# Routing rows in a fused attention and mixture-of-experts kernel: scatters queued ahead of gathers, late rows cleared by plain transfers, and a new split of the last sums

## The reference

```python
x = x + xattn(_layernorm(x), ctx_512, W_k, b_k, ln_gamma, ln_beta)   # softmax of a normalised similarity
...
xf = _layernorm(x).reshape(-1, 256)
top_vals, top_idx = jax.lax.top_k(xf @ router_w.T + router_b, 4)
rw = jax.nn.softmax(top_vals, axis=-1) * 1.8
combine = einsum('tke,tk->te', one_hot(top_idx, 32), rw)
g = silu(einsum('th,eih->tei', xf, gate_w));  u = einsum('th,eih->tei', xf, up_w)
routed = einsum('tei,ehi,te->th', g * u, down_w, combine)
shared = (silu(xf @ shared_gate_w.T) * (xf @ shared_up_w.T)) @ shared_down_w.T
x = x + routed + shared
```

## Time and profile before

| what | us |
|---|---|
| median of 3 runs (lowest and highest) | 178.49 (177.79, 180.09) |
| the profiled execution | 178.13 |
| its span in the trace | 176.0 |
| PE busy | 160.0 |
| DVE busy | 103.1 |
| POOL busy | 82.2 |
| ACT busy | 69.2 |

### The profile page before, as it was taken

How to read it: one execution, slowest core, us unless ns; L and a number is a source line. 1 busy time by engine, 2 the same in 40 slices (tenths; PEclk the granted TensorE clock), 3 DMA queues, 4 the chain that set the end, 5 groups by cost and what they waited for, 6 DMA issues and landing times.

```text
span 176.0 us, 3525 instructions
## 1 busy us (share of the span) xinstructions
PE 160.0 (91%) x1113; PEld 122.9 (70%) x1113; DVE 103.1 (59%) x366; ACT 69.2 (39%) x217; POOL 82.2 (47%) x97
## 2 busy tenths in 40 slices
PE   1999999789989889994998998999999969999993
PEld 0355545356868689994897996899999955338881
DVE  3568598879888426861963776642334434326570
ACT  2024587699765442333033221332234542450020
POOL 6031100000005777787777777774777777710000
PEclk9999999999999999999699999999999999999999
DMA  2899999998991489999469799999999843239964
GB/s 73 243 323 384 326 369 304 343 340 282 295 360 50 113 243 324 334 327 311 153 182 301 219 334 337 299 366 360 352 332 364 248 151 113 93 104 404 406 219 134
DMA packets 22346, 47.60 MB, mean 270 GB/s; under 512 B 3764, under 2 KB 12914, under 8 KB 21682
## 3 DMA queue, kind: packets, MB, share of 16 engines
q1 hardware_dynamic: 18194, 37.35, 64.4%
q0 software_dynamic: 3584, 9.44, 15.6%
q10 hardware_dynamic: 544, 0.52, 0.9%
HBM read 40.44 MB, written 6.86 MB: 269 GB/s over the span
## 4 chain that ended last, share of the span: by engine, by line
PE 40%; POOL 26%; DMA 11%; issue 11%; ACT 7%; DVE 4%; DVEq 0%; POOLq 0%
DMA y_d<-y,to 9%; POOL y_d L485 7%; POOL xn L479 7%; POOL xnT L479 7%; PE ps_x L843 3%; PE ps_g L1010 3%; PE ps_g L836 3%; POOL added_weight L494 2%; DMA xn<-rows_d,idx 2%; PE ps_g L1121 2%; PE ps_h L1121 2%; PE ps_g L1128 2%; POOL y_d L490 2%; PE ps_y L1024 1%; PE ps_y L1026 1%
## 5 line engine op out<-in xcount | busy, mean ns | idle before, releaser
L479 POOL DMA_INDIRECT xn<-rows_d,idx x20 | 20.4, 1021 | 39.1 <-DVE idx L1439 33.3
L485 POOL DMA_INDIRECT y_d<-y,to x32 | 32.7, 1022 | 11.2 <-issue 8.5
L993 PEld LDWEIGHTS ps_g<-xgT,wgu 128*128 128x128 f32 x256 | 31.0, 192 | 1.9 <-ACT xgT L703 0.8
L993 PE MATMUL ps_g<-xgT,wgu 128*128 128x128 f32 x256 | 31.4, 276 | 0.6 <-ACT xgT L703 0.6
L1570 DVE COPY y<-ps_y 128x256 f32<-128x256 f32 x36 | 14.8, 423 | 26.3 <-DMA y_d<-y,to 20.3
L709 ACT ACTIVATE gate<-ps_g 128x256 f32<-128x256 f32 x16 | 6.1, 384 | 50.2 <-PE ps_g L993 50.2
L479 POOL DMA_INDIRECT xnT<-rows_d,idx x16 | 15.4, 964 | 4.9 <-issue 4.6
L993 PE MATMUL ps_h<-xgT,wgu 128*128 128x128 f32 x128 | 16.9, 275 | 0.0
L703 ACT ACTIVATE xgT<-ps_x 128x256 f32<-128x256 f32 x36 | 12.3, 382 | 9.7 <-PE ps_x L979 8.9
L993 PEld LDWEIGHTS ps_h<-xgT,wgu 128*128 128x128 f32 x128 | 15.6, 192 | 0.0
L1024 PE MATMUL ps_y<-wda,hT 128*128 128x256 f32 x32 | 10.0, 428 | 3.4 <-DVE y L1570 3.4
(11 more groups left out here) (265 smaller groups left out, 306.6 us busy)
## 6 DMA issues: line engine op xcount, KB each, us to landing
wgu<-in_w_gu SPq DMA_DIRECT2D x28, 384.0 KB, 4.8
wgu<-in_w_gu SPq DMA_DIRECT2D x5, 1536.0 KB, 13.8
wda<-in_w_da SPq DMA_DIRECT2D x29, 128.0 KB, 5.3
wgu<-y_d SPq DMA_DIRECT2D x6, 512.0 KB, 6.8
wda<-in_w_da SPq DMA_DIRECT2D x5, 512.0 KB, 14.3
wdb<-in_w_db SPq DMA_DIRECT2D x29, 64.0 KB, 5.8
wdb<-in_w_db SPq DMA_DIRECT2D x10, 128.0 KB, 15.5
xnT<-in_xT SPq DMA_DIRECT2D x2, 512.0 KB, 6.4
```

The source lines that it names most:

```text
L479: g.indirect_dma_start(xg[j % RING], None, rows_d, bass.IndirectOffsetOnAxis(ap=idx[:, j:j + 1], axis=0)).then_inc(gathered[j % RING], 16)
L485: g.indirect_dma_start(y_d, bass.IndirectOffsetOnAxis(ap=to[:, j:j + 1], axis=0), y[:, j % 4, :], None).then_inc(scattered[j % 4], 16)
L993: last = t.matmul(bank[:, to_col + i * P:to_col + (i + 1) * P], w_up(2 * m + i, c)[:, at:at + P], xgT[:, i, c, :], start=(c == 0), stop=(c ...
```

## The change

On GpSimd: LEAD goes from 8 to 6, so 12 gathers stand ahead of the loop, and inside the loop the two scatters of pair m come before the two gathers of pair m+6. The four indirect scatters of zeros are gone. In their place SP issues three plain transfers that write zeros over all route rows of the token tiles 5, 6 and 7 (512 KB each), after the second gather has landed, and GpSimd waits for them ahead of its first scatter. The four gathers of weights are split in two and two, and so are the one-hot matrices on DVE. At the end DVE sums five token tiles and PE three, ACT makes one set of diagonal matrices less, and all four output transfers come from SP.

```diff
-LEAD = 8
+LEAD = 6
...
-ON_PE = (1, 3, 5, 7)
+ON_PE = (1, 5, 7)
+ON_DVE = (0, 2, 3, 4, 6)
...
+            sp.wait_ge(gathered[1], 16)
+            yv = y_d[0:ROUTES, :].rearrange("(p k c) h -> p k c h", p=P, c=TOPK)
+            for k in range(EARLY, NT):
+                sp.dma_start(yv[:, k, :, :], wide[:, :].bitcast(F32).unsqueeze(1).to_broadcast([P, TOPK, H])).then_inc(zeroed, 16)
             sp.wait_ge(w4_ready, 1)
...
-            sp.wait_ge(zeroed, 16 * ADDED)
...
-            for q in range(2, 4):
-                sp.wait_ge(final, q + 1)
-                sp.wait_ge(summed_out, q + 1)
+            for q in range(4):
+                last = 2 * q + 1
+                sp.wait_ge(final, sum(k <= last for k in ON_DVE))
+                sp.wait_ge(summed_out, sum(k <= last for k in ON_PE))
...
             pool.wait_ge(to_ready, 1)
+            pool.wait_ge(zeroed, 16 * LATE_TILES)
             for m in range(PAIRS):
+                scatters(m)
                 if m + LEAD < PAIRS:
                     gathers(m + LEAD)
                 if m == PAIRS - SPILL_LEAD:
                     pool.wait_ge(spill_idx_ready, 1)
                 if PAIRS <= m + SPILL_LEAD < PAIRS + OFTEN:
                     gathers(m + SPILL_LEAD)
-                scatters(m)
-                if m == LISTS_AFTER:
+                if m == PAIRS - 5:
                     pool.wait_ge(spill_idx_ready, 1)
-                    clear_rows(0)
-                    clear_rows(1)
-                if m == LISTS_AFTER + 1:
-                    clear_rows(2)
-                    clear_rows(3)
-                if m == LISTS_AFTER + 2:
                     pool.wait_ge(w_table, 32)
-                    for s in range(ADDED):
-                        gather_weight(s)
+                    gather_weight(0)
+                    gather_weight(1)
+                if m == PAIRS - 2:
+                    gather_weight(2)
+                    gather_weight(3)
...
-            weight_matrices(7)
-            ov = out.rearrange("(k p) h -> p k h", p=P)
             for n, k in enumerate(ON_PE):
                 act.wait_ge(y_summed, n + 1)
                 a.activation(xres[:, k, :], sum_bank(k)[:, 0:H], ACT.Copy).then_inc(summed_out, 1)
-                if n < 2:
...
-                    act.dma_start(ov[:, 2 * n:2 * n + 2, :], xres[:, 2 * n:2 * n + 2, :]).then_inc(out_done, 16)
```

More of the change, by code:

```diff
@@ L429, in _ @@
                 spill_loads(OFTEN, SPILL_PAIRS)
-            yv = y_d[0:ROUTES, :].rearrange("(p k c) h -> p k c h", p=P, c=TOPK)
             n_awaited = nc.sync.value_load(awaited[0:1, 0:1], min_val=0, max_val=SPILL_PAIRS)
-            sp.wait_ge(zeroed, 16 * ADDED)
             for u in range(4):
@@ L486, in scatter @@
                     scattered[j % 4], 16)
-            def clear_rows(s):
-                g.indirect_dma_start(y_d, bass.IndirectOffsetOnAxis(ap=to[:, NE + s:NE + s + 1], axis=0), wide[:, :].bitcast(F32), None).then_inc(zeroed, 16)
             def gather_weight(s):
@@ L1494, in spill_experts, with added_one_hot, added_one_hots_ready @@
                 v.scalar_tensor_tensor(awaited[:, :], spills[:, :], 0.0, too_early[:, :], ALU.add, ALU.mult).then_inc(spill_ready, 1)
-            def added_one_hot():
-                link(v.tensor_copy(added_token[:, :], idx[:, NE:NE + ADDED]))
-                dve.wait_ge(added_in, 16 * ADDED)
-                for s in range(ADDED):
+            def added_one_hot(first, end):
+                dve.wait_ge(added_in, 16 * end)
+                for s in range(first, end):
                     made = v.tensor_scalar(added_rows(s), token_row[:, :], added_token[:, s:s + 1], added_weight[:, s:s + 1], ALU.is_equal, ALU.mult)
+                return made
+            def added_one_hots_ready(made):
                 link(made)
@@ L1615, in _ @@
                 if m == PAIRS - 2:
-                    added_one_hot()
+                    link(v.tensor_copy(added_token[:, :], idx[:, NE:NE + ADDED]))
+                    added_one_hot(0, OFTEN)
             with dve.If(n_pairs > 0):
@@ L1646, in last_tiles @@
             def last_tiles():
-                for k in range(0, NT, 2):
+                for k in ON_DVE:
                     add_routes(k)
```

6 lines of the change are left out of this document (2 added, 4 removed).

## The result

The changed kernel takes **171.91 us** (median of 4 runs, 170.45 to 173.63), the kernel before, run beside it, 179.29 us (177.79 to 180.41). The ratio is **0.957, 95% interval 0.944 to 0.969**: faster. The forecast was 170.0, its range 167.5 to 173.5. The profiled execution took 170.45 us with a span of 168.7, against 178.13 and 176.0 before. Executions of one kernel on one chip fall into quicker and slower ones, some per cent apart, and a ratio is taken over the quicker ones of both kernels.

What follows compares the result with a forecast made beforehand. PE and POOL were taken to bound the kernel in turns. Spill work 6.1 us earlier and 2.16 from the split put the sums' end at 165.2; plus 2.62 and 2.13, about 170.0 us, range 167.5 to 173.5.

Steps and rivals of the forecast that it cites:

- The head start: POOL's first scatter at 69.54, 8.56 us sooner; PE's waits between pairs 2 and 15 all gone.
- The count of POOL's queue: POOL's queue to the spill stage: 1.29 us per indirect DMA, first spill gather at 133.4, last scatter at 147.3.
- The clears: SP's plain clears beside the gathers: 5.2 us at 300 GB/s, done at about 66; POOL's wait taken as 0.
- The bumps: Two POOL DMAs beside two-input DVE instructions take longer, together 2.08 us, wherever they fall in a full queue.
- Rival 1: PE becomes the bound: without the two longer POOL DMAs, spill gathers land 2 us sooner, 168.0; chance 0.12.
- The spill stage: PE, ready at 135.4, waits 1.6 to 2.0 us for the spill gathers; what follows on PE moves by -6.1.
- rival 2: PE's wait lowers its clock (1.5 us), POOL waits for clears, scatters land slower: 171.5, up to 173.5; chance 0.20.
- The end: Final sums: one tile less on PE gives 2.16 us; ACT ends at 165.15, DVE at 165.2, last output 2.62 later.
- The sum: Span 167.8 plus 2.13 around it: 170.0 us against 178.13, 4.6% less; chance 0.55 for 168.7 to 171.2.
- rival 3: Little changes: scatters land so late in the full stretch that evictions hold PE as before; 175.3, within 2%; chance 0.09.
- rival 4: Slower: POOL waits for the clears' landing, each microsecond scatter 0 starts after 69.54 adds one; 182; chance 0.04.

Runs made afterwards that it cites:

- the order alone: Kernel before with only GpSimd's order changed (12 gathers first, scatters ahead of gathers), indirect clears and four-and-four split kept: 180.72 us, ratio 1.023.
- the eight clears: Changed kernel with eight plain clears in place of three, GpSimd waiting for all: 177.63 us, ratio 1.002 to the kernel before.
- the earlier spill gathers: Changed kernel with the first two spill gathers right behind pair 11's scatters, four instructions sooner: 172.12 us in one run, kernel before 177.18.
- the clears alone: Kernel before with three plain transfers replacing the four indirect clears, order and split kept: 176.86 to 182.31 us, no ratio; 0.984 on a slow chip.
- L1516 twice: Changed kernel with the two-input DVE instruction of L1516 issued twice in a row, on a slow chip: 206.66 us in one run.

## Why the prediction was right, point by point

The mechanism came about as forecast, stage by stage; that the sum is right to within 0.5 us is in part luck, as the last points say. Times of the prediction are given less the offset of 0.96 us.

- **The head start.** Scatter 0 at 68.58, predicted 68.58. No wait of PE from 60 to 134, full clock, as predicted; `up` of pair 15 at 131.42, predicted 131.5. That the head start is what removes these waits is shown by the order alone, which lost all but 0.81 us of them.
- **The count of POOL's queue.** First spill gather at 132.23 (132.4), last scatter at 147.05 (146.3). The 0.7 us at the end are the 0.66 us wait at 140.60 for an eviction, behind PE's own stall; the prediction had said that no scatter waits there. That the queue must be shorter ahead of it is shown by the order alone, where the spill gather stayed at 85.76 after the first gather.
- **The clears.** Hidden, as taken. The margin is 2.6 us or more, and the eight clears showed that a price comes when they aren't; one for one, as predicted, lies within what those runs allow. The figure of 300 GB/s for the rate was too high (225 for eight), without effect here, but the same figure made the expectation for eight clears too small.
- **The bumps.** Two of them, 0.99 and 0.80 us, together 1.79, predicted 2.08. Rival 1, that they don't come, is out for this trace. That they cost 2.08 wherever they fall in a full queue was too strong: in the order alone, with a full queue, they are 0.70 and 0.18, and the size depends on where POOL's start falls (below).
- **The spill stage.** PE waited 1.98 us, predicted 1.6 to 2.0. Behind it the clock fell: this piece of rival 2 came true, at 1.28 us against 1.5. It belonged in the sum and stood outside it, in a rival. Its other pieces, the wait for clears and slower scatters that hold the evictions, stayed out in the profiled execution.
- **The end.** The split gave 2.15 us, predicted 2.16, and the two ends fell 0.9 us apart. DVE's end, 164.23, is the predicted 164.2, but by another way: SP's loads began at 149.66 and not at 148.8, and DVE's last wait was for the ninth piece at 163.22, where the prediction had DVE busy without a gap from the second tile on. The last output took 3.15 us and not 2.62, for no reason that a run shows.
- **The sum.** 170.0 was forecast and the profiled execution took 170.45. Terms that it missed cancel, and that is luck: the offset (-0.96) and the time around the span (-0.38) against the clock (+1.28) and the last output (+0.53). The profiled execution is also the shortest of the four. The median, 171.91, lies 1.5 us higher; a late gather beside the clears is one thing that differs between executions by that much (1.47 us in the trace of the earlier spill gathers), whether it did so in these four isn't known.
- **Rivals 3 and 4**, the early stall coming back, didn't happen in the changed kernel. The eight clears show that rival 4's is a real mechanism (1.002 of the kernel before). Of rival 3 the clears alone show one landing of 6.76 us in place of 4.99, where scatter 0 had no head start to hide it; that the clears made it slow isn't shown, since the order alone, which has no plain clears, had one of 6.84 (last section).

## What to carry to other kernels

When one queue holds up a faster engine at two places, price the places together: freed at the first alone, the engine runs into the second, and what it gained becomes one long wait with a slow clock behind it (order alone 1.023, order with clears and split 0.957). Count every instruction of the queue ahead of the second place, since in a full queue that count sets when it is reached: with 66 instructions ahead of it the spill gather came 85.76 us after the first gather (order alone), with 60 it came after 78.89. And when a gain is due to a wait being hidden, measure its margin by making the hidden thing larger: eight clears in place of three took all of the gain away. Compare stretches within a trace from a common event such as the first gather, since a delay early on (1.65 us in the earlier spill gathers) can hide what the edit brought later.

## What the runs showed of the hardware that was not expected

**Where the bumps come from.** In each trace two indirect DMAs of GpSimd at most are longer than about 1.0 us beside the 1.22 us DVE instructions with two inputs in SBUF (L1501 and L1516 after, L1509 and L1524 before). Put side by side, these starts give one rule (the plain length of the same kind, 0.95 to 1.00, subtracted):

```
kernel              DVE instruction   POOL start   DVE end less POOL start   longer by
before              75.76 to 76.98    75.82        1.16                      1.03
before              88.37 to 89.60    88.42        1.18                      1.05
changed             74.94 to 76.16    75.04        1.12                      0.99
changed             83.49 to 84.72    83.78        0.94                      0.80
clears alone        76.19 to 77.41    76.23        1.18                      1.04
clears alone        91.32 to 92.54    91.44        1.10                      0.98
order alone         75.13 to 76.35    75.53        0.82                      0.70
order alone         83.07 to 84.30    83.98        0.32                      0.18
eight clears        90.77 to 91.99    91.76        0.23                      0.09
L1516 twice         100.02 to 101.25  99.93        starts ahead              0
L1516 twice         101.28 to 102.51  101.24       starts ahead              0
```

An indirect DMA that starts inside such an instruction is longer by what is left of that instruction less 0.12 to 0.14 us; one that starts even 0.04 us ahead isn't touched, and neither is the DVE instruction, which keeps its 1.23 us. The other traces hold nine more starts inside, 0.08 to 0.99 us longer, that fit within 0.02 us, and eight with less than 0.15 us of the DVE instruction left, which are not longer. A DVE instruction as long with one input, the TENSOR_REDUCE of L1504 after (1.22 us), leaves the indirect DMAs that start inside it at their plain length (0.96 us at 78.62 in the changed kernel). The rows of the order alone and of the eight clears, for example:

```profile
75.53 1.68 POOL L485 DMA_INDIRECT y_d<-y,to  x1 [0.30 <-issue]
...
83.98 1.16 POOL L479 DMA_INDIRECT xn<-rows_d,idx  x1 [0.30 <-issue]
```

```profile
91.76 1.07 POOL L482 DMA_INDIRECT xn<-rows_d,idx  x1 [0.30 <-issue]
```

The Trainium skill says in "Advanced Engine Details and Errata", section VectorE Performance Modes, that DVE's second SBUF port is shared with GpSimd, and that GpSimd's instructions and those of DVE that use two ports block each other. The traces agree as far as GpSimd's side goes, if an instruction with two inputs in SBUF is one that uses both ports, and show it to depend on the moment at which GpSimd starts: 0 to 1.05 us for each.

**Landing in a full stretch.** The gathers into xn issued between 58.8 and 66 us landed after 3.5 us (median) before, 5.0 in the clears alone and 7.7 beside eight clears. The Trainium skill says in "DMA: Bandwidth & Descriptors", section Issuing engines are not separate DMA queues, that transfers from all queues share the 16 engines; these medians agree. For scatters the traces don't single out the clears: scatter 0 of the clears alone released its buffer after 6.76 us, before after 4.99, but the order alone, which has no plain clears, had a scatter started at 97.11 whose buffer came free after 6.84:

```profile
103.95 0.42 DVE L1570 COPY y<-ps_y 128x256 f32<-128x256 f32 x1 [0.65 <-DMA y_d<-y,to]
```

**The clock.** After PE's waits of 1.98, 2.26, 3.95 and 6.95 us the next matmuls ran at the lower level for a while; after waits of 1.49 (before), 1.47 and 1.84 us (earlier spill gathers) they did not. The length of one wait doesn't settle it: in the clears alone two waits of 1.05 and 0.80 us, with two transposes between them, were followed by the lower level from about 146.0 to 149.4.

**Two slow chips.** The same programs took 33 to 40 us longer on two of the chips, in the trace of the changed kernel from about 62 us on. The cause is open.
